# Masking and maximum of the attention scores moved to VectorE, with the projection one image later

## The reference

```python
h = patches(x) @ W + b                        # 196 tokens; layer norm over 3840 shifted pixels
h = concat([h, text_embedding])               # 228 tokens
q = layernorm(h) @ Wq.T + bq                  # 12 heads of 16; k = v = q
w = q @ q.T / 4                               # causal: later keys are masked
w = softmax(w)
h = h + (w @ q) @ Wproj.T + bproj
h = h + ffn(layernorm(h))                     # two quantised linear layers with a GELU
```

## Time and profile before

| | |
|---|---|
| median of 3 runs | 1919.89 us (1918.67 to 1920.64) |
| the profiled execution, its own time | 1918.11 us |
| its span, first to last instruction | 1916.4 us |
| TensorE busy | 1614.7 us (84%), 16574 matrix instructions |
| VectorE busy | 1371.2 us (72%) |
| ScalarE busy | 1171.3 us (61%) |
| GpSimd busy | 1089.9 us (57%) |
| one steady period of the first stage | 19.16 us (806.29 to 825.45 us) |

### The profile page before, as it was taken

One profiled execution on the slowest core, in us unless ns is written; L12 is line 12 of the kernel. 1 busy time (PEld: TensorE's weight loads), 2 busy tenths in 40 slices (PEclk: granted clock), 3 DMA queues, 4 the chain that ended last, 5 costly groups with the idle time before them and its releaser, 6 DMA issues.

```text
span 1916.4 us, 50514 instructions
## 1 busy us (share of the span) xinstructions
PE 1614.7 (84%) x16574; PEld 1363.0 (71%) x16574; DVE 1371.2 (72%) x3151; ACT 1171.3 (61%) x1830; POOL 1089.9 (57%) x1503
## 2 busy tenths in 40 slices
PE   0539999999999999999999999999556666666666
PEld 0438888888888888888888888887445555555555
DVE  3635666666666666666666666666289999999996
ACT  1124555555555555555555555555278888888887
POOL 5035555555555555555555555554177777777775
PEclk9969999999999999999999999999666666666665
DMA  8564656565656565656565656561000000000000
GB/s 103 137 116 69 100 78 99 79 100 78 100 79 100 78 99 80 100 79 99 80 100 78 99 80 100 79 99 26 24 12 22 22 22 22 22 22 22 22 22 26
DMA packets 159967, 132.96 MB, mean 69 GB/s; under 512 B 32558, under 2 KB 151040, under 8 KB 159808
## 3 DMA queue, kind: packets, MB, share of 16 engines
q1 hardware_dynamic: 159168, 131.00, 44.0%
q0 software_dynamic: 768, 1.57, 0.5%
HBM read 118.32 MB, written 11.91 MB: 68 GB/s over the span
## 4 chain that ended last, share of the span: by engine, by line
PE 70%; DVE 14%; issue 5%; SPq 4%; ACT 3%; DMA 2%; POOL 1%; DVEq 1%; ACTq 0%; POOLq 0%
PE ps L1072 24%; PE ps L1154 8%; PE ps L1237 7%; PE ps L1228 7%; DVE ff_st L857 4%; PE ps L1184 4%; PE ps L1216 3%; PE ps L1189 3%; PE ps L1210 3%; PE ps L1314 3%; PE ps L1333 2%; DVE xpix L838 2%; PE ps L1145 2%; PE ps L1135 1%; PE ps L1168 1%
## 5 line engine op out<-in xcount | busy, mean ns | idle before, releaser
L1072 PE MATMUL ps<-w_eff,xpix 118*112 118x193 f32 (+1 forms) x2048 | 457.2, 362 | 21.0 <-POOL side L438 20.4
L1072 PEld LDWEIGHTS ps<-w_eff,xpix 118*112 118x112 f32 (+1 forms) x2048 | 387.8, 253 | 39.8 <-issue 32.8
L915 ACT ACTIVATE probs<-ps,isw 116x688 f32<-116x688 f32 x384 | 298.7, 830 | 175.6 <-PE ps L1216 175.6
L449 POOL TENSOR_TENSOR xsq<-xsq 118x784 f32<-118x784 f32 (+2 forms) x192 | 221.8, 1155 | 293.6 <-ACT xsq L909 283.5
L738 DVE TENSOR_REDUCE nmax<-ps 116x12 bf16<-116x1344 f32 (+2 forms) x192 | 302.2, 1574 | 108.7 <-PE ps L1189 103.8
L524 POOL TENSOR_TENSOR xpix<-probs,g_b 112x192 f32<-112x192 f32 (+1 forms) x512 | 296.5, 609 | 109.0 <-ACT probs L1024 99.7
L469 POOL TENSOR_SCALAR_AFFINE_SELECT probs<-probs 116x464 f32<-116x464 f32 x384 | 268.4, 717 | 46.5 <-ACT probs L915 31.0
L682 DVE TENSOR_SCALAR front_st<-ps 112x1 f32<-112x1 f32 (+1 forms) x128 | 18.3, 152 | 229.2 <-PE ps L1135 218.1
L1314 PE MATMUL ps<-w1t,xpix 96*112 96x384 f16 (+1 forms) x512 | 160.7, 488 | 14.5 <-ACT xpix L1015 13.3
L1154 PE MATMUL ps<-xnT,wq_pad 97*128 97x228 f32 (+1 forms) x768 | 166.0, 365 | 0.0
L1303 PE MATMUL ps<-ident_h,xpix 112*96 112x112 f16 (+1 forms) x256 | 34.9, 281 | 152.9 <-DVE xpix L874 152.9
(11 more groups left out here) (160 smaller groups left out, 3393.3 us busy)
## 6 DMA issues: line engine op xcount, KB each, us to landing
xpix<-in_x SPq DMA_DIRECT2D x192, 196.0 KB
xpix<-in_x SPq DMA_DIRECT2D x192, 195.1 KB
rden<-den_rows SPq DMA_DIRECT2D x256, 85.5 KB, 2.2
out<-xpix SPq DMA_DIRECT2D x64, 87.0 KB
out<-xpix SPq DMA_DIRECT2D x64, 84.0 KB
xpix<-in_x SPq DMA_DIRECT2D x128, 34.1 KB
xpix<-in_x SPq DMA_DIRECT2D x128, 34.0 KB
den<-o_sb SPq DMA_DIRECT2D x256, 2.7 KB
```

The costliest lines, as they stand in the source:

```text
L449: nc.gpsimd.tensor_tensor(out_, a, b, ALU.add).then_inc(s_ssq, 1)
L915: A(probs[0:TB, g, 2 * e:2 * e + 2, :], ps[0:TB, 4 + 2 * e:6 + 2 * e, 0:SK], ACT.Exp, scale=isw[0:TB, 7:8]).then_inc(s_p, 1)
L1072: last = MM(ps_tok[tile][0:P, :], src, w_eff[0:HI, o, :], start=(o == 0), stop=(o == OFFS - 1))
```

## The change

Four things change together.

1. The mask. `score_round` no longer issues the identity products (L1184). The maximum of a row is taken by `tensor_tensor_reduce`, which adds the mask `ahead` (from SBUF, bf16) to the scores in PSUM, writes the sum to a scratch tile and the maximum to one column of `nmax`. It handles one head at a time: 24 such operations for each image, 12 over 112 keys and 12 over 228, in place of 3 reductions. The sign of the maximum goes into the constant `sel`.
2. The rounds. Each of the three is split into two halves of two banks (j0 = 0 and j0 = 2), six in all, and a half waits for the maxima of two halves before it. TensorE's order and the places of the patch products (`CUTS`) change with it.
3. The projection. `normalise`, `project` and `add_attention` work on image n-2, and `o_sb`, `rden` and `den_rows` are doubled. One more period is added at the end. `split_queries` moves behind the layer norm statistics and `add_attention` behind the normalised rows. `invert(n)` moves behind all six maxima.
4. The squares. ScalarE's `inner_squares` moves ahead of `copy_attended(n, 2, 3)` and `copy_turned(n+2)`, and TensorE's `square_turn` moves to the period's end, one image further on.

```diff
-        S1_ROUNDS = [(0, 0, 3), (1, 0, 2), (1, 2, 3)]
+        S1_ROUNDS = [(t, g0, g1, j0) for t, g0, g1 in ((0, 0, 3), (1, 0, 2), (1, 2, 3)) for j0 in (0, 2)]
...
             def turn_denominators(n, b):
                 sp.wait_ge(s_oc, OCS * (n + 1))
...
                 sp.wait_ge(s_row, 16 * (n + 1))
-                after(sp, s_at, n)
...
             def maxima(n, r):
-                t, g0, g1 = S1_ROUNDS[r]
+                t, g0, g1, j0 = S1_ROUNDS[r]
                 k = (TA, TOK)[t]
                 if r == 0:
                     after(dve, s_mt, n)
                 dve.wait_ge(s_s1, MXR * n + r + 1)
-                dst = nmax[0:TB, t, :].rearrange("p (j s) -> p j s", j=PER)[:, :, g0:g1]
-                src = ps[0:TB, 4:4 + PER, 0:(g1 - g0) * k].rearrange("p b (g k) -> p b g k", k=k)
-                V.tensor_reduce(dst, src, AX_X, ALU.max, negate=True).then_inc(s_mx, 1)
+                later = ahead[0:TB, (TA, 0)[t]:(TA, 0)[t] + k]
+                apart(dve)
+                for j in range(j0, j0 + 2):
+                    for g in range(g0, g1):
+                        col = 32 * j + g
+                        at = ((g - g0) * 2 + j - j0) * k
+                        last = V.tensor_tensor_reduce(masked[0:TB, j0 // 2, at:at + k],
+                                                      ps[0:TB, 4 + j, (g - g0) * k:(g - g0 + 1) * k], later,
+                                                      1.0, LOWEST, ALU.add, ALU.max, nmax[0:TB, t, col:col + 1])
+                last.then_inc(s_mx, 1)
...
-            def normalise(n):
-                dve.wait_ge(s_sh, 16 * PER * (n + 1))
+            def normalise(n, b, count):
+                dve.wait_ge(s_sh[b], 16 * PER * count)
                 after(dve, s_z, n)
-                V.tensor_tensor(aT[:, :, :], o_sb[:, :, :], rden[:, :, :], ALU.mult).then_inc(s_at, 1)
+                V.tensor_tensor(aT[:, :, :], o_sb[b][:, :, :], rden[b][:, :, :], ALU.mult).then_inc(s_at, 1)
...
                 def weigh():
                     if prev:
-                        normalise(n - 1)
+                        normalise(n - 2, 1 - b, half)
...
+                if prev:
+                    add_attention(n - 2)
                 if new:
-                    maxima(n + 1, 0)
-                    maxima(n + 1, 1)
+                    for r in range(MXR):
+                        maxima(n + 1, r)
                 if old:
                     invert(n)
-                if new:
-                    maxima(n + 1, 2)
...
                 if newest:
                     edge_squares(n + 3, par, count)
+                    inner_squares(n + 3, par)
                 if old:
-                    copy_attended(n, 2, 3)
+                    copy_attended(n, 1 - b, 2, 3)
                 if newer:
                     copy_turned(n + 2)
-                if newest:
-                    inner_squares(n + 3, par)
...
             def score_round(n, b, r):
-                t, g0, g1 = S1_ROUNDS[r]
+                t, g0, g1, j0 = S1_ROUNDS[r]
                 if r == 0:
                     pe.wait_ge(s_mix, n + 1)
+                    after(pe, s_p, STEPS * n - 1)
+                elif r == 1:
                     after(pe, s_p, STEPS * n)
                 else:
-                    pe.wait_ge(s_mx, MXR * n + r)
-                lo, hi, k, first = (0, TB, TA, 0) if t == 0 else (TA, TOK, TOK, TA)
-                ahead = tri[0:TB, 0:k - first].unsqueeze(1).to_broadcast([TB, g1 - g0, k - first])
-                out_ = [ps[0:TB, 4 + j, 0:(g1 - g0) * k].rearrange("p (g k) -> p g k", k=k) for j in range(PER)]
-                for j in range(PER):
-                    MM(out_[j][:, :, first:], ident_b[0:TB, 0:TB], ahead, start=True, stop=False,
-                       skip_group_check=True)
+                    pe.wait_ge(s_mx, MXR * n + r - 1)
+                lo, hi, k = (0, TB, TA) if t == 0 else (TA, TOK, TOK)
                 for g in range(g0, g1):
-                    for j in range(PER):
+                    for j in range(j0, j0 + 2):
                         rows = slice(32 * j, 32 * j + 32)
-                        last = MM(out_[j][:, g - g0, :], q_mix[b][rows, g, lo:hi], q_hi[b][rows, g, 0:k],
-                                  start=False, stop=True, skip_group_check=True)
+                        last = MM(ps[0:TB, 4 + j, (g - g0) * k:(g - g0 + 1) * k], q_mix[b][rows, g, lo:hi], q_hi[b][rows, g, 0:k],
+                                  start=True, stop=True, skip_group_check=True)
                 last.then_inc(s_s1, 1)
...
-            P1, P2, P3, P4 = 2, 4, 9, 14
+            CUTS = [2, 5, 7, 10, 13]
...
                 if old:
                     scores(n, 1 - b, 0)
-                if newer:
-                    square_turn(n + 2)
                 if new:
                     queries(n + 1)
                 if old:
                     scores(n, 1 - b, 1)
                 if prev:
-                    project(n - 1)
+                    project(n - 2)
                 if old:
                     scores(n, 1 - b, 2)
                     values(n, 0, new)
                     values(n, 1, new)
-                part_of_patches(0, P1)
-                if new:
-                    score_round(n + 1, b, 0)
+                part_of_patches(0)
+                rounds(0, 2)
                 if old:
                     values(n, 2, new)
                 if newer:
                     turn(n + 2)
-                part_of_patches(P1, P2)
+                rounds(2, 3)
+                part_of_patches(1)
+                rounds(3, 4)
                 if new:
-                    score_round(n + 1, b, 1)
                     token_values(n + 1, b, newer)
-                part_of_patches(P2, P3)
-                if new:
-                    score_round(n + 1, b, 2)
-                part_of_patches(P3, P4)
+                part_of_patches(2)
+                rounds(4, 5)
+                part_of_patches(3)
+                rounds(5, 6)
+                part_of_patches(4)
                 if new:
                     turn_maxima(n + 1)
-                part_of_patches(P4, 2 * OFFS)
+                part_of_patches(5)
+                if newest:
+                    square_turn(n + 3)
```

More of the change, by code:

```diff
@@ L38 @@
 NEG = -4.0e10
+LOWEST = -3.0e38
 EPS_LN, EPS_RMS = 1e-5, 1e-6
@@ L99, in build @@
         probs = sb("probs", [128, GROUPS, PER, SK])
-        o_sb = sb("o_sb", [128, GROUPS, TOK])
-        rden = sb("rden", [128, GROUPS, TOK])
+        o_sb = [sb(f"o_sb{i}", [128, GROUPS, TOK]) for i in range(2)]
+        rden = [sb(f"rden{i}", [128, GROUPS, TOK]) for i in range(2)]
         aT = sb("aT", [128, GROUPS, TOK])
@@ L104, in build @@
         den_inv = sb("den_inv", [PER * SPREAD, DENS // SPREAD])
-        den_rows = nc.dram_tensor("den_rows", (PER * SPREAD, DENS // SPREAD), F32, kind="Internal").ap()
+        den_rows = [nc.dram_tensor(f"den_rows{i}", (PER * SPREAD, DENS // SPREAD), F32, kind="Internal").ap()
+                    for i in range(2)]
         g1_b = sb("g1_b", [128, DIM])
@@ L214, in build @@
         s_row = sem("inverses_stored")
-        s_sh = sem("inverses_broadcast")
+        s_sh = [sem(f"inverses_broadcast{i}") for i in range(2)]
         s_v = sem("values_copied")
@@ L755, in add_attention, with step_images @@
                 last.then_inc(s_h2, 1)
-            def step_images(n, b, prev=True, old=True, new=True, newer=True):
+            def step_images(n, b, half, prev=True, old=True, new=True, newer=True):
                 def weigh():
                     if prev:
-                        normalise(n - 1)
+                        normalise(n - 2, 1 - b, half)
                 def split():
@@ L765, in split @@
                         split_queries(n + 1, b)
-                def add():
-                    if prev:
-                        add_attention(n - 1)
                 if newer:
                     links[:] = [0, (n + 2) * V_FRONT]
-                    front(n + 2, weigh, split, add)
+                    front(n + 2, weigh, split)
                 else:
@@ L922, in copy_turned, with copy_attended @@
                   ACT.Copy).then_inc(s_xts, 1)
-            def copy_attended(n, lo, hi):
+            def copy_attended(n, b, lo, hi):
                 act.wait_ge(s_o, GROUPS * n + hi)
-                after(act, s_at, n)
-                A(o_sb[:, lo:hi, :], ps_o[:, lo:hi, :], ACT.Copy).then_inc(s_oc, 1)
+                after(act, s_at, n - 1)
+                A(o_sb[b][:, lo:hi, :], ps_o[:, lo:hi, :], ACT.Copy).then_inc(s_oc, 1)
             def high_queries(m, b):
@@ L1140, in turn @@
                 pe.wait_ge(s_xn, n + 1)
-                after(pe, s_h2, n - 2)
+                after(pe, s_h2, n - 3)
                 for c in range(2):
@@ L1239, in project, with part_of_patches, rounds @@
                 last.then_inc(s_z, 1)
-            P1, P2, P3, P4 = 2, 4, 9, 14
+            CUTS = [2, 5, 7, 10, 13]
```

(11 more changed lines are left out.)

65 lines of the change are left out of this document (33 added, 32 removed).

## The result

The changed kernel takes 1960.1 us (median of 4 runs, 1958.97 to 1961.73), the one before 1919.53 us on the same chip: a ratio of 1.021 (1.019 to 1.023), slower. The profiled execution has a span of 1958.5 us against 1916.4. The attention stage ends (the last `add_attention`) at 1431.7 us and not at 1388.9, 42.8 us later; the FFN behind it takes as long as before. A steady period, from one `turn_maxima` to the next and averaged over the stage, grew from 19.19 to 19.89 us, 0.70 us; over about 60 periods that is the whole loss.

What follows compares the result with a forecast made beforehand. TensorE alone bounded the kernel before; VectorE's maxima would then set the period: 11.87 + D (8.39) = 20.26 us. 61 x (20.26 - 19.16) = 67 us and about 4 us more on 1918.11 give about 1990 us, range 1930 to 2090.

Steps and rivals of the forecast that it cites:

- The likeliest case: VectorE works through all 24 maxima without a pause, then turn_maxima: a period of 20.26 us, 1990 us; chance 0.50.
- rival 1: Copied norms bind alone ahead of token_values, the accumulator nearly free (o at most 0.13): period 19.58 us, 1948 us; chance 0.25.
- The maxima: VectorE's 24 operations start 9.36 us into the period and last 8.39 us; 2.46 us follow turn_maxima: period 20.26 us.
- o: Cost beyond its elements of each of VectorE's 24 maxima operations: 0.07 + 0.09 = 0.16 us.
- D: Duration of all maxima on VectorE: 4.25 + 0.3 + 24 x 0.16 = 8.39 us.
- Queries read late: VectorE's last query read, behind the layer norm statistics, ends at 6.6 us, so TensorE's values(n, 0) waits 0.28 us.
- Norms copied late: ScalarE's inner_squares delays the copies, so token_values cannot start before 13.10 us: alone a period of 19.58 us, 0.42 more.
- TensorE's own work: Mask products (1.19 us) go, half rounds and gaps come: 18.45 to 19.33 us a period, 0.7 us gained at most.
- What costs nothing: Doubled o_sb, rden and den_rows, the moved invert and the extra projection at the end: no cost; slack covers invert.

Runs made afterwards that it cites:

- the version without waits: Changed kernel with split_queries first on VectorE, the copies first on ScalarE, and two patch products moved ahead of the third half: 1895.6 us, 0.988 of the kernel before.
- both orders put back: Changed kernel with split_queries again ahead of the layer norm statistics and the copies again ahead of inner_squares: 1922.7 us, 1.0024 of the kernel before.

## Why the prediction was right, and where its steps failed

**The side and the range.** Slower by 2.1%, 1960.1 us against a forecast of 1990 in 1930 to 2090. The likeliest case was the wrong one, and that the time lies even in this case's own range (1955 to 2050) is luck. The period is not set by VectorE working through all 24 maxima up to `turn_maxima`. It is set by rival 1's late queries and then, not by rival 1's copied norms, but by the first six maxima ahead of the third half; the norms come 0.15 us behind. Rival 1's sum was 19.58 us, 1948 us; of the 0.31 us that it lacks, 0.29 are the late queries, priced at 0.28 and measured at 0.57 us.

**The maxima (the step that failed).** I took 0.07 us for an operation's start and 0.09 for the accumulator's read. The read is there, 85 ns long, but it starts together with the next operation and costs nothing: o is 0.08 us and not 0.16. With it my sum gives D = 4.25 + 0.3 + 24 x 0.08 = 6.47 us and a period of 11.87 + 6.47 = 18.3 us, below the 19.58 us of the norms. Two more steps of this path were off. The maxima began 9.93 us into the period and not 9.36: the first products start at 9.37 and not at 9.06, behind the late `values`, which this path of the sum had on time, and 0.56 us pass from them to the first maximum, not 0.30. And VectorE does not work without a pause: in the period shown it waits 0.36 and 0.80 us for the last two halves. ScalarE's 0.09 us did not carry over to VectorE. The rule in the Trainium skill, "VectorE: DVE Perf Modes", section "Two Vector instructions with no wait between them", that an operation with an accumulator output is two instructions, agrees with the trace (1257 reads for 1257 operations). The estimate worked out from that page's errata table, 0.185 us, does not. Its section "The DRAIN you can't avoid" says that the next operation does not start until the pipe is empty, and adds what the prediction left out, that an operation which is not held starts earlier; here they start 0.20 us apart at a length of 0.27.

**Queries read late (right, too small).** 0.28 us was predicted and 0.57 measured. `front` begins 0.19 us into the period and not at 0.0, for the scores follow the squares without a gap, and the last read of the queries ends 6.75 us behind it in place of 6.6. The experiment that undoes only this gave back 0.54 us a period, 32 us. It is the main cost of the change, and the prediction had it as a minor one.

**Norms copied late (right, but not what held `token_values` back most).** `token_values` was forecast 13.10 - 6.73 = 6.37 us behind `values`; it came 6.45 behind, and 6.44 us went from there to the period's end, against 6.48 in the sum. The last agreement is in part luck: the squares take 0.50 us (812.62 to 813.12) and not 0.33, and the 0.26 us of idle time ahead of `scores(n, 0)`, which the sum kept, is gone behind them. The experiments show how little room there is: undone in the changed kernel it returns about 7 us, made alone in the kernel before it costs 39.

**TensorE's own work (right).** 18.45 to 19.33 us were given for a period without waits; the version without waits has 18.83. Taking the mask products (1.19 us) away pays only if something else covers the maxima: alone, their removal lost 10 us.

**What was left out.** The third half's wait for the first maxima was in no term of the sum. With both orders put back it is 0.61 us where 0.17 is usual, and all that keeps that kernel from being faster: without it the period is 0.46 us shorter.

**What costs nothing.** The projection and the double buffers cost nothing and gained nothing. The moved `invert` was costed at nothing too; the squares alone show that it has a use beside the early squares, for in its old place it then waits 1.85 us in the middle of the maxima. The moved `add_attention` was not costed at all; the trace puts about 0.15 us a period on it once the queries are read early.

**Parts.** From the kernel before to the changed one, in us a period: late queries +0.54, early squares +0.10, wait for the first maxima +0.46, and TensorE's own work 18.83 - 19.19 = -0.36, together +0.74; measured +0.70. The first two overlap by 0.04 (0.60 us with both undone).

## What to carry to other kernels

Work that is removed from the bounding engine is gained only as far as no other engine was being waited for behind it: before taking it away, read in the timeline how long ahead each of its waits is satisfied, and put other work there (here two patch products, 27 us). When operations are reordered on an engine off the path, ask which of them releases the bounding engine; a pair of VectorE's operations moved behind the layer norm statistics cost 0.54 us a period, more than the whole change gains (0.36) when everything else is in a good order. And try parts alone and together: of the three parts tried alone one was neutral and two lost, and the mask paid only with halves and another order around it.

## What the runs showed that was not expected

An accumulator read on VectorE cost nothing here behind its own operation: reads of 85 ns start together with the next operation, at 0.20 us a step for 112 elements and 0.32 for 228, while ScalarE's read took 0.09 us of its own.

The FFN stage ran at different granted clocks of TensorE in the two kernels, and in the same time. Windows of the changed kernel and then of the one before: start and end, length, busy time of the engines with their instructions, clock, DMA share, GB/s:

```profile
1430.00:1958.00 528.00, 313.15 (x2311) 256.04 (x2309) 473.76 (x1356) 438.06 (x769) 384.15 (x578) 0.77 0.07 21
```

```profile
1390.00:1916.00 526.00, 350.53 (x2304) 284.79 (x2304) 469.12 (x1351) 442.38 (x769) 377.62 (x578) 0.64 0.07 21
```

The clock is 0.77 of full speed in one and 0.64 in the other, TensorE is busy 313 us against 351, and the stage still ends 527 us after the last `add_attention` in both (1958.5 - 1431.7 and 1916.4 - 1388.9). So TensorE does not bound it; VectorE is busy for 474 of 528 us. The clock does not go with the kernel: the executions of the kernel before have mean clocks from 0.883 to 0.917 of full speed and take 1914 to 1923 us, among them 1914.4 us at 0.915 and 1914.5 us at 0.884. Why it differs behind the same code stays open.
